# Attention masks on GpSimd: single score banks of the square and mixed groups join the alternation

## The reference, cut to what matters

```python
scores = jnp.einsum('bhsd,bhtd->bhst', q, k) / math.sqrt(float(DH))
mask = jnp.tril(jnp.ones((S, S), dtype=scores.dtype))
scores = scores * mask
scores = jnp.where(scores == 0.0, -jnp.inf, scores)
attn = jax.nn.softmax(scores, axis=-1)
out = jnp.einsum('bhst,bhtd->bhsd', attn, v)
```

## Time and profile before

| | |
|---|---|
| median of 3 runs | 2175.01 us (2171.84 to 2177.18) |
| the profiled execution | 2171.33 us |
| its span, first to last instruction | 2169.6 us |
| mean granted TensorE clock | 0.978 |
| attention, first exp to last weighing | 142 us to 1346 us |

### The profile page before, as it was taken

The page is one execution under the profiler, slowest core; times in us unless marked ns, Lnnn a source line. Parts: engine busy times, 40 slices in busy tenths (PEclk is TensorE's granted clock), DMA queues, the critical chain, the costliest instruction groups (busy, mean ns, idle before and its releaser), DMA issues. The chain is left out here.

```text
span 2169.6 us, 30271 instructions
## 1 busy us (share of the span) xinstructions
PE 1948.0 (90%) x10299; PEld 838.4 (39%) x10427; DVE 1704.7 (79%) x2499; ACT 1422.9 (66%) x1921; POOL 927.8 (43%) x823
## 2 busy tenths in 40 slices
PE   7989899989999899999899997799999877999997
PEld 4542222222222222222222222566665535777775
DVE  6879999999999999999999998468887863333332
ACT  5769999989999989999889997354544421111110
POOL 5854544433334333434333343235565553333333
PEclk9999999999999999999999999799999988999999
DMA  6642311022212022216300100110000123443441
GB/s 206 211 154 43 54 23 30 3 51 41 32 23 32 25 45 42 35 20 210 107 25 13 35 22 8 59 40 29 30 30 30 36 90 99 103 105 98 104 101 24
DMA packets 123390, 133.73 MB, mean 62 GB/s; under 512 B 33753, under 2 KB 117554, under 8 KB 122544
## 3 DMA queue, kind: packets, MB, share of 16 engines
q1 hardware_dynamic: 108656, 117.86, 20.0%
q0 software_dynamic: 14592, 14.08, 3.7%
HBM read 96.85 MB, written 50.63 MB: 68 GB/s over the span
## 5 line engine op out<-in xcount | busy, mean ns | idle before, releaser
L1270 DVE SCALAR_TENSOR_TENSOR arena<-ps_s,arena 128x1024 f32<-128x1024 f32 (+1 forms) x1071 | 1146.7, 1138 | 41.5 <-ACT arena L1233 33.7
L1233 ACT ACTIVATE arena<-ps_s 128x1024 f32<-128x1024 f32 (+1 forms) x1194 | 1041.0, 935 | 109.5 <-PE ps_s L1176 96.2
L1176 PE MATMUL ps_s<-arena 128*128 128x512 bf16 (+3 forms) x2176 | 581.0, 365 | 103.8 <-DVE arena L1270 77.1
L1192 PE MATMUL ps_o<-arena,values 128*32 128x512 f32 (+3 forms) x4608 | 565.7, 568 | 9.1 <-ACT arena L1222 4.3
L1282 POOL TENSOR_SCALAR arena<-arena 128x512 f32<-128x512 f32 x123 | 236.1, 1920 | 500.2 <-ACT arena L1238 500.1
L1176 PEld LDWEIGHTS ps_s<-arena 128*128 128x128 bf16 x2304 | 155.1, 97 | 694.2 <-DVE arena L1270 532.1
L1837 ACT ACTIVATE arena<-t_ps_four 128x320 f32<-128x320 f32 (+1 forms) x96 | 42.0, 437 | 314.9 <-PE t_ps_four L1720 314.9
L2166 POOL DMA_INDIRECT out<-values,slot_ids x80 | 123.5, 1544 | 238.9 <-DVE values L2086 210.5
L1720 PE MATMUL t_ps_four<-arena 128*128 128x320 f32 (+1 forms) x768 | 211.4, 435 | 0.6 <-DVE arena L2047 0.6
L1192 PEld LDWEIGHTS ps_o<-arena,values 128*32 128x32 f32 x4608 | 94.1, 108 | 233.0 <-issue 185.4
L2059 DVE TENSOR_TENSOR arena<-t_ps_four,arena 128x320 f32<-128x320 f32 (+1 forms) x96 | 47.2, 492 | 168.7 <-ACT arena L1837 168.7
(11 more groups left out here) (201 smaller groups left out, 1711.0 us busy)
## 6 DMA issues: line engine op xcount, KB each, us to landing
arena<-parts_dram SPq DMA_DIRECT2D x320, 64.0 KB, 2.2
parts_dram<-arena SPq DMA_DIRECT2D x32, 384.0 KB, 3.3
arena<-parts_dram SPq DMA_DIRECT2D x24, 512.0 KB, 7.1
slots_in_dram<-in_empty_slots SPq DMA_DIRECT2D x10, 1040.0 KB, 24.6
arena<-slots_in_dram SPq DMA_DIRECT2D x16, 650.0 KB, 4.8
arena<-in_L_ffn_w_gate SPq DMA_DIRECT2D x16, 352.0 KB, 3.1
arena<-in_L_ffn_w_up SPq DMA_DIRECT2D x16, 352.0 KB, 3.6
arena<-in_L_attn_x SPq DMA_DIRECT2D x8, 512.0 KB, 4.1
```

The source lines that it names most:

```text
L1176: last = pe.matmul(ps_s[:, unit.bank + i, p.at:p.at + p.width], m.k_stack[:, group.g % 2 * HG + p.head, p.kt * P:p.kt * P + P], q_stack[:, ...
L1192: last = pe.matmul(ps_o[32 * p.head:32 * p.head + 32, p.w0:p.w0 + p.width], m.values_flat[:, at:at + 32], probs[:, job.at % PROB_BANKS, p. ...
L1233: act.activation(probs[:, unit.slot:unit.slot + n], ps_s[:, unit.bank:unit.bank + n], ACT.Exp, scale=1.0 / DH ** 0.5).then_inc(exped, 1)
L1270: dve.scalar_tensor_tensor(p, ps_s[:, unit.bank:unit.bank + n], 0.0, p, ALU.not_equal, ALU.mult).then_inc(bank, 1)
```

## The change

A job of a square or mixed group can now be "shared" where before only a job of a full group could. A single place that follows another single becomes shared, whatever its group, unless it is a half group. The second edit makes POOL wait, before it zeroes the triangles of a diagonal group, for its own multiply of a shared job of that group.

```diff
@@ Plan.place_jobs
-                    shared = singles % 2 == 1 and jobs[taken].group.kind == "full"
+                    shared = singles % 2 == 1 and jobs[taken].group.kind != "half"
                     singles = 0 if shared else 1
                     self.units.append(Unit(n, at, "shared" if shared else "single", jobs[taken:taken + 1]))
@@ phase_attend, gpsimd
                     for group in plan.closing(unit):
 
                         pool.wait_ge(bank, plan.masked_through(group))
+                        if plan.shares_through(group):
+                            pool.wait_ge(last_masked, plan.shares_through(group))
                         for lo, hi in group.squares():
```

## The result

The changed kernel takes 2192.53 us (median of 4 runs, 2190.98 to 2194.75) against 2175.8 us before (4 runs): a ratio of 1.0081, 95% interval 1.0063 to 1.0098. It is slower by 16.7 us, twice the 8.5 us that were forecast, and 1.5 us above the stated range. Its profiled execution took 2194.75 us, with a span of 2192.8.

What follows compares the result with a forecast made beforehand. DVE, busy 193.5 of 200 us, was taken as nearest to full in attention. Saved masks -3.8, late weighings +7.4 and gates' steps +4.9 gave +8.5 us: 2171.33 to 2179.8 profiled, 2175.0 to 2183.5 median; range 2172 to 2191.

Steps and rivals of the forecast that it cites:

- Part 1: Attention: 12 masks leave DVE as shared places go from 123 to 135, each worth 0.32 us, gaining 3.8 us.
- Part 2: POOL's multiply ahead of the diagonal triangles makes nine mixed weighings late, 8.45 us in sum, 7.4 us after slack.
- What absorbs it: Finished exps waiting for DVE hide 0.5 us each in blocks 20 and 21, so 1.0 us comes off the lateness.
- rival 3: Stalls compound: a shared place behind a stall has ACT copy while DVE is empty; about +15 us, 2190; chance 0.11.
- Part 3: Renumbered gates' steps land before the square closings of blocks 2 and 3: 2.3 and 2.6 us late, cost 4.9 us.
- The sum: Whole kernel: -3.8 + 7.4 + 4.9 = +8.5 us, shifting the end whole; median 2175.0 becomes 2183.5 us.
- The page against the rows: POOL's one-bank mask: trace gives 1.92 + 1.28 us, the skill page's factor of two 1.4 us and some -2.7 in sum.
- Rival 1: At the nine mixed weighings the lateness is absorbed: +1.1 us (2176.1), or -3.8 (2171.2) if gates' steps are too; chance 0.30.
- rival 2: In attention DVE's whole saving arrives, 12 masks of 0.60 us: -7.2 us, 2167.8; chance 0.04.

Runs made afterwards that it cites:

- kernel 1: The changed kernel with the five steps on the gates put back behind units 47, 87, 123, 159 and 195; 2183.2 us, ratio 1.0045 to before.
- kernel 9: The kernel before with the ten shared places right behind a turn made singles; attention 1.0 us shorter, whole 2174.5 us.
- kernel 6: The kernel before with one extra POOL compare ahead of the mixed group's selects in eight blocks; attention 8.3 us longer, whole 2183.7 us.
- kernel 5: The kernel before with, at nine blocks, the mixed group's single shared and the shared place behind it a single; attention +9.4 us, whole 2181.8 us.
- kernels 13 to 15: On kernel 5, second place behind each mixed group shared for the third, 2187.9 us; kernel before with nine first places unshared, 2178.1; that with the same move, 2177.9.
- kernel 7: The kernel before with two extra POOL compares ahead of the square group's select in eight blocks; attention 22.6 us longer, whole 2192.2 us.
- Kernel 13: Kernel 5 with the second place behind each of the nine mixed places shared in place of the third; attention +12.0 us against before, whole 2187.9 us.

## Why the prediction was wrong, by its own steps

The direction, the places and their order were right, the size was half. The terms of the sum that were mis-sized:

- **Part 1, the count** of 12 net masks was right. **Its value was not**: "12 x 0.32 = 3.8 us". What is left of it in kernel 1 is 0.7 us (10.6 for attention, against 11.3 for its nine blocks with a late mixed weighing). The step that failed is that I priced a number of units without looking at where they go. The planner's new alternation has 22 shared places behind a turn instead of 10, so all twelve net additions lie where kernel 9 shows that sharing saves nothing. Away from turns there are 113 in both kernels.
- **Part 2, POOL's chain**, was right in order, place and length: nine waits, in the nine blocks named, 5.55 us from the square select to the weighing in block 4 where the working gives 5.56, and the square groups nearly free (0.2 us at three of them, 0.6 in the last block). The lateness was worked out as 8.45 us and measured as 10.8. PE's time of arrival, taken from the kernel before, was wrong: in four of the nine blocks kernel 1 waits 0.3 to 0.4 us longer than kernel 5, and there the shift of the alternation had changed the place ahead. Where the rest comes from (in blocks 27 to 29 both kernels wait 0.3 us more than was worked out) is open.
- **"What absorbs it"** failed: I took 1.0 us off, and kernel 6 shows 0.2 us in each of the two blocks with slack and 8.3 us of loss for 8.6 us of waits. On the contrary, rival 3's mechanism adds to it: a shared place behind the stall, 2.5 us in sum (kernels 13 to 15). So the nine places cost 11.3 us in kernel 1, not 7.4.
- **Part 3, the gates' steps**: the waits were 1.92 and 2.80 where 2.3 and 2.6 stood, 4.7 against 4.9 in sum. The cost was 7.3. What the sum had no term for is the granted clock, which fell to 1.2 GHz behind both.
- **The sum**: -0.7 + 11.3 + 7.3 = 17.9 us of attention, against -3.8 + 7.4 + 4.9 = 8.5. Of the 9.4 us between them 3.1 are part 1, 3.9 part 2 and 2.4 part 3. The nine stretches of kernel 1 are read against another pattern of places, so 11.3, and with it 0.7, is good to some 1 us. Between the medians the change is 16.7 us.
- **The page against the rows.** The measured 3.28 us for compare and multiply, not the page's factor of two, was the right choice: POOL took 1921 and 1277 ns again.
- **The rivals.** Rival 1 is refuted by kernel 6, rival 2 by DVE's idle time. Rival 3 had the nearest number, 2190, but partly by luck: its mechanism is real, and gives 2.5 of the 9.4 us that were missing.

## What to carry to other kernels

An engine that is idle more than half of the time can still be late: before giving it work ahead of something that another engine waits for, add up its queue in program order from the moment the first input is ready, and count what hangs on a counter that the change renumbers. A saving measured on one place of a pattern holds only where the same engine sets the pace; ask for each place that is gained which engine does. And a stall on TensorE may cost more than it lasts.

## What was not expected of the hardware

TensorE's granted clock fell behind waits of 1.92 and 2.80 us in the changed kernel, and of 1.73, 2.86, 2.86 and 2.26 us in kernel 7, but not behind 1.73 (block 13) and 2.24 us (three blocks), nor behind 1.71 and 1.72 us in kernel 6. The kernel before has waits of 1.66 and 1.88 us of its own, at 755.7 and 1057.3 us, with the clock at 1.00. Each fall cost 0.8 to 1.5 us beyond the wait.

A long wait is not needed either. This is what came before and in the slow stretch of kernel 5 in block 9, and then its busy time:

```profile
470.22 0.99 PE L1179 MATMUL ps_s<-arena 128*128 128x512 bf16 x3 [0.47 <-DVE arena L1273]
471.95 0.60 PE L1179 MATMUL ps_s<-arena 128*128 128x512 bf16 x2 [0.74 <-DVE arena L1273]
473.08 0.86 PE L1179 MATMUL ps_s<-arena 128*128 128x512 bf16 x2 [0.53 <-DVE arena L1273]
473.88 1.94 PE L1195 MATMUL ps_o<-arena,values 128*32 128x512 f32 x8
```

```profile
473.00:477.00 4.00, 3.92 (x16) 0.60 (x20) 3.51 (x4) 2.21 (x4) 3.19 (x2) 0.57 0.01 0
```

No wait there passes 0.74 us, and the fall still cost 1.6 us. Kernel 13 shows the same fall at the same place, the other kernels none. The Trainium skill (TensorE: Matmul & The Clock Gate, "What's actually happening") states that the slow clock is the default and that activity releases it. The trace agrees as far as it goes: 1.00 before the waits and 0.50 to 0.52 after some of them, though PE was 100% busy in the slow stretch of block 3. Equal waits gave both outcomes, so a sum can only carry this as a risk with its price.
